# Ten additions of the SAGE layer moved from VectorE to GpSimd, and the diagonal of the count matrix taken out during the FFN

## What is computed

```python
edge_index = jnp.stack([src, dst])
x = x + _L0_gnn_ref(_layernorm(x, axis=-1), edge_index, L0_gnn_W, L0_gnn_b)      # three GCN layers
x = x + _L0_ffn_ref(_layernorm(x, axis=-1)[None], ...)[0]                         # small FFN on two nibbles
x = x + _L1_gnn_ref(_layernorm(x, axis=-1), edge_index, W_l, b_l, W_r, gamma, beta)
x = x + _L1_ffn_ref(_layernorm(x, axis=-1)[None], ...)[0]                         # shared and routed experts

def _layernorm(x, axis=-1, eps=1e-05):
    m = jnp.mean(x, axis=axis, keepdims=True)
    v = jnp.var(x, axis=axis, keepdims=True)
    return (x - m) / jnp.sqrt(v + eps)

def _L0_gnn_ref(x, edge_index, W, b):
    src = jnp.concatenate([edge_index[0], loops]); dst = jnp.concatenate([edge_index[1], loops])
    ...

def _L1_gnn_ref(x, edge_index, W_l, b_l, W_r, gamma, beta):      # x is the normalised input here
    agg = jax.ops.segment_sum(x[src], dst, num_segments=n)
    cnt = jax.ops.segment_sum(jnp.ones((src.shape[0],), x.dtype), dst, num_segments=n)
    mean_agg = agg / jnp.maximum(cnt, 1.0)[:, None]
    h = mean_agg @ W_l.T + b_l + x @ W_r.T
    mu = jnp.mean(h, axis=0)
    var = jnp.var(h, axis=0)
    h = (h - mu) * jax.lax.rsqrt(var + EPS) * gamma + beta
    return jax.nn.relu(h) + x
```

## Time and profile before

| | us |
|---|---|
| median of 3 runs | 863.76 (862.98 to 864.32) |
| the profiled execution | 863.68, span 861.70 |

### The profile page before, as it was taken

How to read it: one execution, slowest core, us unless ns; L and a number is a source line. 1 busy time by engine, 2 the same in 40 slices (tenths; PEclk the granted TensorE clock), 3 DMA queues, 4 the chain that set the end, 5 groups by cost and what they waited for, 6 DMA issues and landing times.

```text
span 861.7 us, 13555 instructions
## 1 busy us (share of the span) xinstructions
PE 792.2 (92%) x3933; PEld 618.9 (72%) x3934; DVE 528.1 (61%) x943; ACT 321.1 (37%) x542; POOL 139.2 (16%) x186
## 2 busy tenths in 40 slices
PE   3899899999999989997999969988989999999983
PEld 1556788888888876676888857877867777777761
DVE  7787832421441487887023675897487878778751
ACT  1563512521431204533211253332255555556531
POOL 2000000000000210000000500212134343545321
PEclk9999899999999998998999998987999999999997
DMA  7500000000000010000101103002998949874632
GB/s 173 162 1 2 1 1 1 1 0 1 1 1 1 31 52 0 1 1 1 49 1 45 72 2 120 1 0 90 335 339 271 312 94 361 268 201 73 155 60 35
DMA packets 32292, 71.39 MB, mean 83 GB/s; under 512 B 4387, under 2 KB 4637, under 8 KB 32243
## 3 DMA queue, kind: packets, MB, share of 16 engines
q1 hardware_dynamic: 24480, 53.31, 17.8%
q0 software_dynamic: 6272, 14.68, 8.5%
q10 hardware_dynamic: 1491, 2.73, 0.9%
HBM read 96.53 MB, written 12.72 MB: 127 GB/s over the span
## 4 chain that ended last, share of the span: by engine, by line
PE 77%; DVE 15%; issue 4%; ACT 2%; DMA 1%; DVEq 1%; ACTq 0%; POOL 0%; POOLq 0%
PE PS L1125 22%; PE PS L1159 10%; PE PS L1378 9%; PE PS L1425 8%; PE PS L1257 5%; PE PS L1067 4%; PE PS L1372 4%; PE PS L1200 3%; PE PS L1410 3%; PE PS L1049 2%; PE PS L1356 1%; PE PS L1387 1%; PE PS L1098 1%; DVE XN L1495 1%; PE PS L1302 1%
## 5 line engine op out<-in xcount | busy, mean ns | idle before, releaser
L1125 PE MATMUL PS<-CTR,YH 125*128 125x500 f32 (+1 forms) x480 | 164.4, 358 | 2.3 <-DVE YL L1683 2.3
L1125 PE MATMUL PS<-CTR,YL 125*128 125x500 f32 (+1 forms) x480 | 163.8, 356 | 0.0
L1125 PEld LDWEIGHTS PS<-CTR,YH 125*128 125x128 f32 x480 | 91.6, 191 | 15.6 <-DVE YL L1683 2.6
L1125 PEld LDWEIGHTS PS<-CTR,YL 125*128 125x128 f32 x480 | 91.8, 191 | 13.0
L2006 DVE TENSOR_TENSOR W1L<-WB,W1H 128x1152 fp32r<-128x1152 f32 x56 | 74.0, 1356 | 17.1 <-issue 10.1
L1425 PE MATMUL PS<-WB,YF 128*128 x168 | 78.6, 605 | 2.5 <-issue 1.7
L1710 DVE TENSOR_TENSOR ZL<-PS,ZH 128x500 fp32r<-128x500 f32 (+1 forms) x36 | 21.1, 591 | 90.4 <-ACT ZH L789 90.4
L1378 PE MATMUL PS<-W1H,XGH 128*128 128x384 f32 x168 | 73.2, 436 | 0.0
L976 ACT CAST W1H<-WB 128x1152 fp32r x56 | 64.2, 1151 | 16.3 <-issue 11.0
L1378 PE MATMUL PS<-W1L,XGH 128*128 128x384 f32 x168 | 57.3, 341 | 0.0
L1378 PE MATMUL PS<-W1H,XGL 128*128 128x384 f32 x168 | 56.9, 339 | 0.0
(11 more groups left out here) (393 smaller groups left out, 1638.9 us busy)
## 6 DMA issues: line engine op xcount, KB each, us to landing
WB<-in_w SPq DMA_DIRECT2D x28, 1536.0 KB
WB<-in_w SPq DMA_DIRECT2D x28, 768.0 KB
WB<-in_b SPq DMA_DIRECT2D x28, 384.0 KB
X<-in_x SPq DMA_DIRECT2D x1, 2240.0 KB
xn_dram<-XN SPq DMA_DIRECT2D x1, 2240.0 KB
WNEXT<-in_W SPq DMA_DIRECT2D x2, 1024.0 KB, 10.1
SR<-in_sw SPq DMA_DIRECT2D x1, 1536.0 KB, 7.7
out<-X ACTq DMA_DIRECT2D x1, 1120.0 KB
```

The lines of the kernel that those rows point to most:

```text
L1125: mm = nc.tensor.matmul(dest, lhs, rhs, start=(t == 0 and h == 0), stop=(t == NT - 1 and h == 1))
```

## The change

The ten additions of XN to X leave VectorE. GpSimd does them, tile by tile, each once that tile of XN is written (`xn_ready`), ahead of the memset in its queue. The subtraction of the identity from CTR is called in the FFN loop, behind the statistics of chunk 2. VectorE gets one wait, for all ten additions, ahead of its next use of X.

```diff
@@ gpsimd, behind the split of the FFN's weights
             pool.tensor_tensor(w2l[0:GU + 1], w2f, f32(w2h[0:GU + 1]), ALU.subtract).then_inc(ffn_weights, 1)
 
+            for t in range(NT):
+                pool.wait_ge(xn_ready, t + 1)
+                pool.tensor_tensor(X[0:NP, t, :], X[0:NP, t, :], XN[0:NP, t, :], ALU.add).then_inc(xn_added, 1)
+
             pool.wait_ge(mean_ready, FT * len(SPLITS))
@@ vector, in the loop over the FFN's chunks
                     v.bn_stats(stats[0:NP, t, 0, :], X[0:NP, t, 0:OUT0])
                     v.bn_stats(stats[0:NP, t, 1, :], X[0:NP, t, OUT1:D])
+                if c == 2:
+                    self_loops(ALU.subtract, loops_ready)
                 if c == 3:
                     split_weight(3, WRAW[:, :, :])
@@ vector, in front of the neighbour means
             for t in range(NT):
                 low_part(LAYERS * NT + t, t, XN[0:NP, t, :])
-            self_loops(ALU.subtract, loops_ready)
-            for t in range(NT):
-                v.tensor_tensor(X[0:NP, t, :], X[0:NP, t, :], XN[0:NP, t, :], ALU.add).then_inc(xn_added, 1)
@@ vector, behind the statistics of the hidden values
             scale_shift(FT - 1)
+            dve.wait_ge(xn_added, NT)
             for t in range(NT):
                 dve.wait_ge(back_ready, t + 1)
```

## The result

Over 17 runs each the kernel before has a median of 863.51 us (860.47 to 866.74) and the changed one 866.03 us (863.96 to 869.19): a ratio of 1.0037, with a 95% interval of 1.0024 to 1.005. By the two medians that is 2.5 us slower; the ratio, which isn't the quotient of the medians, comes to 3.2 us (2.1 to 4.3). The forecast was 2.7.

The account below looks back on a forecast made before the run. TensorE was taken to bound the kernel, stalled 7.20 us at the fifth SAGE group by VectorE's additions. Normalisation delay 8.7 + clock 1.2 - 4.99 - 2.21 = +2.7 us: median 866.5 us, range 859.5 to 868.8.

Parts of the forecast that it names:

- What bounds: TensorE's stall at the fifth SAGE group, waiting through ScalarE for VectorE's additions: 4.99 idle + 2.21 slow clock = 7.20 us.
- The diagonal: Ten VectorE instructions, 2.08 us, moved into the FFN, where idle time and slack cover them: cost 0.
- Taking turns: GpSimd additions and VectorE normalisations exclude one another and alternate from the second normalisation on: +8.7 us; chance 0.70.
- (a): Rival: VectorE keeps the port through its normalisations, additions begin at 383.5; about 860.1 us, chance 0.12.
- (b): Rival: the port goes over at every second normalisation, four additions inside, +4.3 us there; 861.4 us, chance 0.10.
- (c): Rival: no exclusion between normalisations and GpSimd additions, the whole 7.20 us won; 856.5 us, chance 0.08.
- The size of a turn: An addition of 1.14 and a normalisation of 0.40 make a 1.54 us pair; eight pairs end the tenth normalisation at 392.2.
- the lower bound of 7.1: Least delay of the normalisations in turns, with 1.08 us for an addition: 8 x 1.34, +7.1 us.
- The clock: TensorE's 8 us idle before ZL lowers the clock to 1.2 GHz and slows the last transposes: +1.2 us, bounds 0.3 and 2.5.
- The sum: Whole kernel: 8.7 + 1.2 - 4.99 - 2.21 = +2.7 us, giving 866.4 profiled and 866.5 median.
- all behind moves along: Everything after the SAGE layer's affected groups shifts by the same amount, TensorE without a wait.
- The deciding point: For a gain, with 1.2 for the clock, the normalisations' delay must stay under 6.0 us, a pair under 1.21 us.

Follow-up runs that it names:

- e7: Changed kernel with GpSimd adding tiles 0 to 4 after all ten normalisations, VectorE adding the other five behind YL: 857.35 us, ratio 0.9924 to before.
- e8: Changed kernel without GpSimd's additions; VectorE forms the residual from X and the statistics, ScalarE's wait for additions goes: 856.26 us, ratio 0.9917 to before.
- e9: Kernel before with 18 filler products on TensorE in the hole ahead of the fifth SAGE group: 864.54 us, ratio 1.0013 to before.
- e3: Changed kernel with every GpSimd addition waiting for all ten normalisations: 861.50 us, ratio 0.9965 to before.
- e10: Changed kernel with 30 filler products on TensorE while it waits for the normalisations: 869.54 us, ratio 1.0072 to before.
- e2: Changed kernel with the diagonal back behind YL, additions still on GpSimd: 865.52 us, ratio 1.0019 to before.
- e11: Changed kernel unaltered, run and profiled a second time: 865.13 us, ratio 1.0013 to before.
- e5: Changed kernel with the first four GpSimd additions starting with their tile, the other six after all ten normalisations: 861.84 us, ratio 0.9974 to before.

## Why the prediction was right, and where it was not

**What bounds.** Right. The stall at the fifth group was priced at 4.99 + 2.21 = 7.20 us. SAGE without it is 103.12 (changed), 103.16 (e7) and 103.20 (e8) instead of 110.59, which is 7.4 to 7.5 (the second profiles, 102.74 and 110.11, give 7.4 too); the filler of e9 puts 2.31 on the clock's part.

**The diagonal.** Right at 0. It ends at 358.70 where I had worked out 359.16, and 0.35 of that is the earlier start of the whole trace; TensorE does not wait for what stands behind it.

**Taking turns.** Right in kind, and it decided the sign. From the second normalisation on the engines alternated one for one. Rivals (a), (b) and (c) are out: no addition waited for the tenth normalisation, none skipped a turn, and none lay over a normalisation for nothing. e3 shows besides that the changed kernel would have been faster if (a) had held.

**The size of a turn.** Mis-sized. I put a pair at 1.14 + 0.40 = 1.54 us; it is 1.41. The 1.28 for an addition was right (1.27 for the last of the changed kernel, which meets only ZL; in e3 and e7 five in a row are 1.24 apart), so the mis-sized step is what each engine takes off its length at a change of turn. Put against additions alone, 1.24 apart, a normalisation adds 1.41 − 1.24 = 0.17 us where I had 0.40, while the 1.14 for an addition's turn was 0.10 too short; this split is by subtraction, and only the 1.41 and the 1.24 are measured. With full lengths a pair would be 1.28 + 0.54 = 1.82, so 0.41 lies outside the turns, where I took off 0.28. Eight pairs make 7.6 where I had 8.7; the lower bound of 7.1 rested on a shorter addition, which did not happen.

**The clock.** 0.92 by e10, where I had taken 1.2 with bounds 0.3 and 2.5. The clock did fall, but part of the low stretch lay in the idle time (388.9 to 391.64).

**The sum.** By the terms measured it is 7.6 + 0.9 − 7.45 = +1.1 us, against my +2.7: the way in was priced 1.3 too long and the stall 0.3 too short. The first pair of profiles gives 121.38 − 120.29 = +1.1 for way in and SAGE together, the second 121.00 − 120.67 = +0.3, where a stretch of low clock at 373 us made the filler ahead of the transposes last 10.38 us instead of 8.75 and added 0.86 to before's way in. So the closeness of the median's +2.5 to the forecast is in part luck: the layer explains about 1 us of it. I had written that all behind moves along; the other 1.5 arises there, in a rest that varies by 3 to 4 us in either kernel, and whether the change shifts that variation or the two sets of 17 runs merely differed stays open; e2 (+0.9 by the medians, +1.6 by the ratio) and e11 (+1.6 and +1.1) point to a smaller loss than 2.5. The sign is clear in the first 17 runs and in e2, not in e11.

**The deciding point.** I wrote that the delay must stay under 6.0 us for a gain. e5 puts it to use: with four early additions the way in is 4.45 longer, under the 6.0, and the kernel gains 1.7 us.

## What to carry to other kernels

In these runs work given to GpSimd was free only beside VectorE instructions with one of their two operands in PSUM: five additions beside such subtractions cost neither engine anything (6.12 against 6.11 us), while eight beside normalisations on the path cost 7.6 us, and five beside subtractions of two SBUF operands 5.6. Release such work by what VectorE does next and not by when its inputs are ready. And before moving an instruction to another engine, ask whether it can be rewritten so that nobody waits for it: the residual from the statistics won the whole stall (0.9917) on VectorE itself.

## What was unexpected in the hardware

- GpSimd and VectorE alternate with a period of 1.41 us (normalisation) or 1.71 us (two SBUF operands). That is less than the sum of what each needs alone, 1.24 + 0.46 = 1.70 and 1.24 + 0.60 = 1.84, so the exclusion does not cover whole instructions as the records show them. The Trainium skill, "SBUF — State Buffer", section "Who interferes with whom", has the loser blocked for the whole instruction of the other; an estimate by that rule from these figures would be 1.70 for the first. The measured 1.41 decides.
- Filler to hold the clock can cost more than it saves, even when it fits its hole: e10 regained 0.92 us and lost 4.97 us of idle time and a cold stretch 80 us later, in a place that it never touched; e9 regained 2.31 us in the layer and nothing at the end. Where e10 lost it is shown, but why isn't tested; in e9 neither is.
- Two profiles of one kernel differ by 3 to 4 us in the last 350 us, most of it in the loop over experts, where the clock is nearly always full, and not in stretches of low clock. A pair of profiles can price a place, but not a difference of 2 us at the end.
